# A two-pass attention and feed-forward kernel: a second buffer for the down forms, staged weights loaded in two parts ahead of the codes, two slices cast by VectorE, and another order of loads at two seams

## What is computed

```
x = x + xattn(layernorm(x), ctx, ctx)        # softmax over 8 heads of 128 channels
h = layernorm(x)
gate, up = h @ Wg.T, h @ Wu.T                # Wg, Wu: 2752 x 1024, W = level[code] * scale
y = x + (silu(gate) * up) @ Wd.T             # Wd: 1024 x 2752
```

## Time and profile before

| | before |
|---|---|
| runs | 1632.52, 1638.27, 1640.72 us |
| the profiled execution | 1641.01 us, its span 1639.3 us |
| mean granted TensorE clock | 0.954 |
| busy: PE / VectorE / ScalarE / POOL | 91% / 58% / 61% / 4% |
| DMA queue share of 16 engines | 55.4% |

### The profile page before, as it was taken

The page is one execution under the profiler, slowest core; times in us unless marked ns, Lnnn a source line. Parts: engine busy times, 40 slices in busy tenths (PEclk is TensorE's granted clock), DMA queues, the critical chain, the costliest instruction groups (busy, mean ns, idle before and its releaser), DMA issues.

```text
span 1639.3 us, 18807 instructions
## 1 busy us (share of the span) xinstructions
PE 1492.3 (91%) x6804; PEld 1230.7 (75%) x6804; DVE 958.4 (58%) x1479; ACT 997.8 (61%) x1268; POOL 60.9 (4%) x99
## 2 busy tenths in 40 slices
PE   7999999999999998878879787798649999999999
PEld 7888888888888886656667666676538888888787
DVE  6986444443443332655556555565428878878765
ACT  5787998888888874666557565576413333333321
POOL 3343000000000000000000000000000000000000
PEclk9999999999999999988899988898879999999999
DMA  6554576666665767446455554555694443444341
GB/s 225 174 174 137 183 241 208 214 204 207 220 209 172 265 193 276 149 159 186 167 174 174 173 191 158 177 172 176 240 366 175 152 169 128 167 155 148 123 141 78
DMA packets 135708, 303.23 MB, mean 185 GB/s; under 512 B 9792, under 2 KB 57920, under 8 KB 130368
## 3 DMA queue, kind: packets, MB, share of 16 engines
q1 hardware_dynamic: 135616, 302.03, 55.4%
HBM read 189.27 MB, written 112.72 MB: 184 GB/s over the span
## 4 chain that ended last, share of the span: by engine, by line
PE 65%; DMA 14%; ACT 7%; DVE 7%; issue 3%; SPq 2%; ACTq 0%; DVEq 0%
PE bank L1494 10%; PE bank L1495 10%; PE bank L1493 10%; PE bank L1582 8%; PE bank L1584 7%; PE bank L1583 7%; DMA wf_scratch<-F 7%; DMA F<-w_scratch 5%; PE bank L1441 3%; PE bank L1539 2%; ACT F L808 2%; DVE R L1144 2%; PE bank L1540 2%; PE bank L1541 2%; DVE F L1144 2%
## 5 line engine op out<-in xcount | busy, mean ns | idle before, releaser
L1539 PE MATMUL bank<-R 128*128 128x512 f32 x604 | 253.5, 420 | 107.7 <-ACT F L885 63.3
L738 ACT ACTIVATE F<-F 128x1024 f32<-128x1024 f32 x294 | 311.9, 1061 | 9.3
L1493 PE MATMUL bank<-R 128*128 128x512 f32 x688 | 268.2, 390 | 0.0
L1494 PE MATMUL bank<-R 128*128 128x512 f32 x688 | 268.0, 389 | 0.0
L1495 PE MATMUL bank<-R 128*128 128x512 f32 x688 | 268.0, 389 | 0.0
L1540 PE MATMUL bank<-R 128*128 128x512 f32 x604 | 249.6, 413 | 0.0
L1541 PE MATMUL bank<-R 128*128 128x512 f32 x604 | 248.3, 411 | 0.0
L1144 DVE TENSOR_TENSOR F<-F 128x256 f32<-128x256 f32 (+2 forms) x305 | 169.4, 582 | 130.3 <-ACT F L857 127.5
L957 ACT COPY F<-bank 128x512 f32<-128x512 f32 x120 | 70.5, 588 | 268.9 <-PE bank L1584 268.1
L1539 PEld LDWEIGHTS bank<-R 128*128 128x128 f32 x604 | 122.5, 203 | 143.2 <-ACT F L885 67.1
L1144 DVE TENSOR_TENSOR R<-F,R 128x512 fp32r<-128x512 f32 (+2 forms) x215 | 164.9, 785 | 16.7 <-ACT R L872 16.5
(11 more groups left out here) (116 smaller groups left out, 2132.6 us busy)
## 6 DMA issues: line engine op xcount, KB each, us to landing
wf_scratch<-F SPq DMA_DIRECT2D x70, 512.0 KB, 3.1
F<-in_gu_scales SPq DMA_DIRECT2D x86, 256.0 KB, 3.9
inter_scratch<-F SPq DMA_DIRECT2D x84, 256.0 KB, 2.5
F<-w_scratch SPq DMA_DIRECT2D x21, 1024.0 KB, 8.2
FR<-wf_scratch SPq DMA_DIRECT2D x21, 1024.0 KB, 6.0
F<-in_gu_codes SPq DMA_DIRECT2D x41, 512.0 KB, 4.0
w_scratch<-F SPq DMA_DIRECT2D x41, 512.0 KB, 4.6
F<-inter_scratch SPq DMA_DIRECT2D x40, 512.0 KB, 3.7
```

Source lines behind the costliest of these rows:

```text
L738: nc.scalar.activation(y, y, ACT.Prelu, bias=bias, scale=scale, alpha=alpha).then_inc(bent, 1)
L1493: pe.matmul(dst, hi, xh[:, tb, t, :], start=(t == 0), stop=False)
L1494: pe.matmul(dst, hi, xl[:, tb, t, :], start=False, stop=False)
L1539: pe.matmul(dst, hi, xform[i][:, 0, j, :], start=a, stop=False, skip_group_check=not start)
```

## The change

- The down forms get a second buffer, in a slice of `R2` that stage 2 does not use, with a semaphore each: form k waits for form k-2.
- `load_staged` becomes `load_gate` and `load_up`, 512 KB each. In a pass both stand ahead of the codes and scales. `load_gate(p+1)` waits for `wform_lo(p, 3)` and the sums of p, `load_up(p+1)` for `wform_lo(p, 5)`.
- Slices 5 and 6 are cast by VectorE (`BY_DVE`), and its order is 5, 4, 6.
- `weight_sums(p + 1)` stands between `form_lo(p, 0)` and `form_lo(p, 1)` (was behind both).
- At the start of stage 2, `load_gate(1)` goes ahead of `load_xform(5)` and `load_up(1)` between `load_xform(5)` and `load_xform(6)` (was behind both, and behind codes and scales).
- At the end of stage 2, two `load_y` instead of six stand ahead of the last stores; `load_stage(1)`, whose buffer is now f(18), follows the store of pair_out(21, 0); the other six `load_y` come after `load_w(0, 6)`. The wait for all inter stores moves to VectorE's `lo_s(1)`, whose destination is now slice 14 of `FR`, and to SP ahead of the last rows.

The diff, cut to its core (a rename of the local `made` to `which` is left out):

```diff
+        wdform = [form, [R2[:, 7 * N + q * WIDE:7 * N + (q + 1) * WIDE] for q in range(2)]]
+        wdform_out = [f(12), R2[:, 7 * N:8 * N].bitcast(F32)]
...
+        def made(p, i, those=range(NP)):
+            order = (0, 1, 2, 3, 5, 4, 6)
+            own = [j for j in order if j in those]
+            until = order[:order.index(i) + 1]
+            return sum(j in own for q in range(p) for j in used(q)) + sum(j in own for j in used(p) if j in until)
+        BY_ACT, BY_DVE = (0, 1, 2, 3, 4), (5, 6)
...
-        pieces = [[R2[:, 7 * N:8 * N], R2[:, 2 * AB:2 * AB + N]], [R2[:, 4 * N:5 * N], FR[:, 18 * N:19 * N]]]
+        pieces = [[R2[:, 7 * N:8 * N], R2[:, 2 * AB:2 * AB + N]], [R2[:, 4 * N:5 * N], FR[:, 14 * N:15 * N]]]
-        stage = [f(15), f(14)]
+        stage = [f(15), f(18)]
...
-            def load_staged(p):
+            def load_gate(p):
                 c = chunk_of(p)
                 if p:
-                    sp.wait_ge(wfl_ready, nth(p - 1, NP - 1))
...
+                    sp.wait_ge(wfl_ready, made(p - 1, 3))
+                    sp.wait_ge(ws_ready, p)
+                sp.dma_start(staged[:, 0:N], w_dram[GU - 1 if c == FULL else 2 * c]).then_inc(gate_in, 16)
+            def load_up(p):
+                if p == FPOS:
+                    return
+                if p:
+                    sp.wait_ge(wfl_ready, made(p - 1, 5))
+                sp.dma_start(staged[:, N:2 * N], w_dram[2 * chunk_of(p) + 1]).then_inc(up_in, 16)
...
+            load_gate(1)
             sp.wait_ge(up_done, ups_until(2 * FPOS + 3))
             load_xform(5)
+            load_up(1)
             load_xform(6)
             store_block(2 * FPOS + 3)
             for p in range(POS):
                 if p:
                     store_pair_out(p - 1, 1)
+                if p and p + 1 < POS:
+                    load_gate(p + 1)
+                    load_up(p + 1)
                 next_item(WN + 2 + p)
...
-                if p + 1 < POS:
-                    load_staged(p + 1)
                 for tb in range(4):
                     store_form(p, tb)
...
-                    for m in range(6):
+                    for m in range(2):
                         load_y(m)
                 store_pair_out(p, 0)
-            sp.wait_ge(pair_done, nth(FULL, NP - 1))
+            load_stage(1)
             store_pair_out(FULL, 1)
...
             load_w(0, 6)
-            for s in range(2):
-                sp.wait_ge(inter_stored[s], 2 * IN1)
-            load_stage(1)
-            for m in range(6, NM):
+            for m in range(2, NM):
                 load_y(m)
...
-                wait(act, form_stored, 16 * k)
-                nc.scalar.copy(form[0], src).then_inc(fh_ready, 1)
+                wait(act, form_stored[k % 2], 16 * (k // 2))
+                nc.scalar.copy(wdform[k % 2][0], src).then_inc(fh_ready, 1)
...
-                for i in range(4, NP):
-                    wform_hi(p, i)
+                wform_hi(p, 4)
...
-                dve.wait_ge(wfh_ready, nth(p, i))
+                if i in BY_DVE:
+                    dve.wait_ge(*((pair_done, nth(p - 1, i)) if p else (up_done, ups_until(NB1 - 1))))
+                    dve.wait_ge(ws_ready, p + 1)
+                    nc.vector.tensor_copy(wslice[i][:, 0], src).then_inc(wfd_ready, 1)
+                    dve.wait_ge(wfd_ready, made(p, i, BY_DVE))
+                else:
+                    dve.wait_ge(wfh_ready, made(p, i, BY_ACT))
...
-                for i in range(4, NP):
-                    wform_lo(p, i)
+                wform_lo(p, 5)
+                wform_lo(p, 4)
+                wform_lo(p, 6)
...
                 form_lo(p, 0)
+                if not last:
+                    weight_sums(p + 1)
                 form_lo(p, 1)
...
-                weight_sums(p + 1)
...
-                wait(pe, wfl_ready, nth(p, i))
+                pe.wait_ge(wfl_ready, made(p, i))
```

More of the change, by code:

```diff
@@ L355, in xattn_ffn @@
         wd_stored = sem("wd_stored")
-        t_ready, fh_ready, fl_ready, form_stored = sem("t_ready"), sem("fh_ready"), sem("fl_ready"), sem("form_stored")
+        t_ready, fh_ready, fl_ready, form_stored = sem("t_ready"), sem("fh_ready"), sem("fl_ready"), [sem(f"form_stored{b}") for b in range(2)]
         gate_done, up_done, silu_ready = sem("gate_done"), sem("up_done"), sem("silu_ready")
@@ L582, in _ @@
                     sp.wait_ge(fw_stored, 16 * SLICES)
-                    load_staged(0)
+                    load_gate(0)
+                    load_up(0)
             store_block(2 * FPOS - 1)
@@ L605, in _ @@
                     store_rest(0)
-                    sp.wait_ge(form_stored, 16 * 2 * NP)
+                    for b in range(2):
+                        sp.wait_ge(form_stored[b], 16 * NP)
                     load_w(0, 0)
-                if p + 1 < POS:
-                    load_staged(p + 1)
                 for tb in range(4):
@@ L662, in _ @@
                     sp.wait_ge(wd_stored, 32)
+                    for q in range(2):
+                        sp.wait_ge(inter_stored[q], 2 * IN1)
                     sp.wait_ge(product_done, NP * g + 1)
@@ L844, in form_hi @@
             def form_hi(c, tb):
-                made = form_of(c, tb)
-                if made is None:
+                which = form_of(c, tb)
+                if which is None:
                     return
-                k, _, _, src, _ = made
+                k, _, _, src, _ = which
                 if k == 0:
@@ L949, in hi_s @@
                 act.wait_ge(s_ready, g + 1)
+                if g == 0:
+                    act.wait_ge(form_stored[1], 16 * NP * KW // 4)
                 wait(act, product_done, NP * (g - 1))
@@ L1157, in form_lo @@
             def form_lo(c, tb):
-                made = form_of(c, tb)
-                if made is None:
+                which = form_of(c, tb)
+                if which is None:
                     return
-                k, _, _, src, _ = made
+                k, _, _, src, _ = which
+                hi, lo = wdform[k % 2]
                 dve.wait_ge(fh_ready, k + 1)
-                sub(form[1], src, form[0].bitcast(F32)).then_inc(fl_ready, 1)
+                sub(lo, src, hi.bitcast(F32)).then_inc(fl_ready, 1)
             def wide(v):
@@ L1197, in weight_sums @@
             def weight_sums(p):
-                dve.wait_ge(staged_in, 16 * (p + 1))
+                dve.wait_ge(gate_in, 16 * (p + 1))
                 if p == FPOS:
@@ L1305, in lo_s @@
                 dve.wait_ge(hs_ready, g + 1)
+                if g == 1:
+                    for s in range(2):
+                        dve.wait_ge(inter_stored[s], 2 * IN1)
                 sub(sform[g % 2][1], stemp.rearrange("p (a n) -> p a n", a=2), sform[g % 2][0].bitcast(F32)).then_inc(ls_ready, 1)
```

34 lines of the change are left out of this document (14 added, 20 removed).

## The result

The changed kernel takes **1499.08 us** (median of 4 runs, 1496.39 to 1500.02) beside 1638.02 us for the kernel before on the same chip. The ratio is 0.9153, 95% interval 0.9127 to 0.9179: faster by 8.5%. The forecast was 1504 us. The profiled execution took 1500.02 us, its span is 1498.3 us. Its span is 141.0 us under that of the execution profiled before, where the sum had 134.7.

What follows compares the result with a forecast made beforehand. Stage 2 was taken as bound by waits in a circle, for `snap2` (63.3 us) and `c22_sum` (20.5). Gains 108.2 + 12 + 12.5 + 2 = 134.7 us from 1641.0 make 1506.3, less 2.7 to the runs' median: 1504; range 1486 to 1538.

Steps and rivals of the forecast that it cites:

- passes 1 to 19: Stage 2's full passes: 483.5 us would become 19 x 19.04 plus 13.5 of waits, 108.2 us gained.
- pass 0: First pass of stage 2: earlier load for pass 1 cuts 31.2 us to 19.0, gaining 12 (9.5 if x form late).
- half pass and pass 21: End of stage 2: five products end at 33.7 us against 46.2, 12.5 us gained.
- start of stage 3: Steps 0 and 1: the 21.21 us hole shrinks, but a new wait appears; 2 us gained (0 to 6).
- The size of the wait in even passes: Product 6 waits 1.5 us in each of 9 even passes, 13.5 us; bounds 0 and 2.3 each.
- the landing is at T + 12.5: Even passes: tb 0's form store lands 12.5 us after T, when SP has issued the second inter store.
- The load in two: Staged weights in two halves land 6.6 us after SP issues the second inter store (between 6.0 and 8.2).
- Casts and sums at nothing: In the passes, moving two casts to VectorE and its sums earlier was costed at nothing.
- the circle binds: Rival for stage 2: later landings make the circle bind instead of TensorE, 40 us instead of 13.5; 1530 to 1539; chance 0.25.
- slower: Rival for stage 2: VectorE, in order, waits for a late load; at 18 us landing, 1695 us; chance 0.02.
- the second buffer does not free ScalarE: Rival for stage 2: stores land too late for both buffers, only the load's move counts; about 1600; chance 0.03.
- The queue lets nothing wait: Rival: forms and load land a little earlier, no even pass waits, stage 3's seam gives 6; 1486; chance 0.2.

Runs made afterwards that it cites:

- Experiments 1 to 3: Changed kernel with one form buffer, 1594.64 us; kernel before with only the second form buffer, 1601.13 us; changed kernel with gate and up loads behind the codes, 1596.77 us.
- Experiment 10: Changed kernel with the store of form tb 0 ahead of codes and scales in even passes: 1494.20 us, ratio 0.9120 to the kernel before.
- experiments 4 and 5: Changed kernel with slices 5 and 6 cast by ScalarE again, 1499.54 us; changed kernel with the sums behind the second form's low half again, 1498.80 us.
- experiment 7: Changed kernel with gate and up of pass 1 loaded behind both x forms, codes and scales again: 1510.87 us.
- experiment 9: Changed kernel with the y loads spread, six of them behind the stage load for step 2: 1484.88 us, ratio 0.9069 to the kernel before.
- experiment 3: Changed kernel with gate and up loads of passes 2 to 21 behind codes and scales again, both form buffers kept: 1596.77 us.

## Why the prediction was right

| term | forecast | measured |
|---|---|---|
| passes 1 to 19 | 108.2 | 115.3 |
| pass 0 | 12 | 12.4 |
| half pass and pass 21 | 12.5 | 11.9 |
| start of stage 3 | 2 | 0.8 |
| ahead of stage 2 | 0 | 0.6 |
| sum | 134.7 | 141.0 |

The first three are differences between first matmuls (482.0 - 366.7, 31.4 - 19.0, 47.4 - 35.5). The forecast was reckoned from the cuts of the earlier trace rows, which have 1.5 us too much in passes 1 to 19 and 1.2 too little in the half pass with pass 21. Stage 2 starts 0.6 us earlier, at 631.9 instead of 632.5, and what is left of 141.0 is put down to the start of stage 3. There product 4 of step 1 came 35.0 us behind the end of stage 2 (1053.2 to 1088.23) instead of 38.0, and later matmuls at the half clock give 2 us of that back: step 2 begins after 41.2 us instead of 42.0.

**The second buffer and the earlier load: right.** `snap2` is no longer waited for, `c22_sum` of an even pass is late next, and `form_hi` of tb 2 waits for a landing behind it, all as named. Experiments 1 to 3 show that it takes both. Of the 120.2 us by which the 19 passes were above 361.8, TensorE was idle for 85.4; the rest goes with the clock of 0.90.

**The size of the wait in even passes: the term that was off.** The step "the landing is at T + 12.5" was taken from the order before by keeping its 13.3 us and filling one hole. In the nine even passes `form_hi` of tb 2 began at T + 10.4 to T + 11.8, so the landing was 0.7 to 2.1 us sooner; T + 11.7 in pass 12 is among the latest. Measured are 4.9 us in 7 passes where 13.5 in 9 were forecast, the longest single wait 1.0 us where 1 to 2 was given as a sign. The 19 passes were thus to take 375.3 us and took 366.7, 8.6 less, of which the table shows 7.1 because the forecast began from 483.5. The half pass and stage 3 take 1.8 back, pass 0 and the earlier start of stage 2 add 1.0, which leaves the 6.3 by which the sum was low.

The landing is not all of it. The forecast had ScalarE late into an odd pass and "back on time behind it", at T 2.0 us into the even pass. Behind the odd passes 5 and 15, whose load let the sums begin only at T + 7.2 and T + 8.2, it was not: T came 3.0 and 3.2 us into passes 6 and 16, and these have the two longest waits; pass 15 itself, an odd one, waits as well. Together these three have 3.2 of the 4.9 us. Experiment 10 shows that the form's landing is still what starts it: it moves that store alone, T is then 1.98 us into 16 of the 19 passes, and the waits go.

**The load in two: right** (T + 6.6 forecast, T + 5.6 to T + 6.3 measured in even passes). What the Trainium skill says of 1 MiB and of the fixed cost per DMA ("DMA: Bandwidth & Descriptors", Rules for kernel authors and the section on latency) would have added some 9 us by the prediction's reckoning; the trace has none of them.

**Casts and sums at nothing: right** (experiments 4 and 5, 364.5 and 364.1 us beside 366.7).

**Pass 0: right**, 12.4 us (experiment 7: 11.6). The load had landed by 641.20 where 641 was forecast; of the terms of that sum, the 2 us added to the transfer time are shown apart by no run.

**The half pass with pass 21: 1.8 us short.** They were to take 33.7 us and took 35.5. Pass 21 starts 12.62 us behind the half pass, where 12.7 was forecast, and product 2 waits there as named:

```profile
1037.60 0.50 PE L1571 MATMUL bank<-R 128*128 128x512 f32 x1 [1.58 <-ACT F L897]
```

But product 6 of pass 21 waits as well, 1.5 us for `c22_sum` (at 1050.33), which I had not worked through.

**Stage 3: right in its mechanism.** The gain went into a new wait in step 1, since the queue stays full (1.02 before and after, 1.00 with the order undone) and the same bytes stand ahead of the stage for step 2. Only fewer bytes ahead of it help, and experiment 9 shows what that is worth: 12.3 us behind the end of stage 2.

The rivals: *the circle binds* and *slower* needed later landings than were measured; *the second buffer does not free ScalarE* fell with the waits for `snap2`. *The queue lets nothing wait* came half true: 12 of the 19 passes waited for nothing.

## What to carry to other kernels

Where two engines and a queue wait for each other in a circle, price the waits together: removed alone, each brought here less than a third of what both bring. Follow a transfer's place in the queue back to what is issued ahead of it, and put first what the next step needs first; once a stretch has the queue at 1.0, what helps is to move bytes from ahead of the transfer that is waited for to behind it, even if the queue stays full. Count a hole of a few microseconds at more than its idle time if matmuls behind it start at twice their distance.

## What was not expected of the hardware

- Holes of 3.29 and 3.43 us left eight matmuls at the half clock behind them (0.63 us long, 0.43 apart), some 1.7 us more each. In the three kernels of experiments 1 to 3 such runs and the slow first matmuls make 26 to 33 us. The length of a hole alone does not tell whether one follows: behind the 2.81 us in the kernel before and behind 2.65 us in experiment 3 only the first matmul was longer (0.50), while 1.83 us in the kernel before left eight slow ones. The run need not begin at once: behind a hole of 3.86 us in experiment 3 the first six starts were 0.23 to 0.34 us apart, and only then 0.43. The 1.83 us hole, and the one of 2.65 us:

```profile
786.30 0.65 PE L1539 MATMUL bank<-R 128*128 128x512 f32 x1 [1.83 <-DVE F L1236]
786.75 0.63 PE L1540 MATMUL bank<-R 128*128 128x512 f32 x1
787.18 0.63 PE L1541 MATMUL bank<-R 128*128 128x512 f32 x1
```

```profile
1009.56 0.50 PE L1571 MATMUL bank<-R 128*128 128x512 f32 x1 [2.65 <-DVE F L1263]
1009.90 0.40 PE L1572 MATMUL bank<-R 128*128 128x512 f32 x1
```

- Two loads of 512 KB, issued 0.58 us apart, let the sums begin at T + 5.6 to T + 6.3 in even passes, one of 1 MB at T + 5.9 to T + 7.0. The gate half is issued about 0.7 us sooner, and a second fixed cost does not show.
- VectorE's cast of 128x512 took 0.42 us, near the lower of the two bounds given for it (0.35 and 0.69).
